# A GNN with residual layer norms: in the last stage GpSimd's two powers of a block are one instruction on 128x16 elements, for blocks three places apart

## The reference

```python
out = _ffn(h, W1u, b1u, W2u, b2u)            # h = [x, agg], 128 features to 64; two GELUs
sq = jnp.sum(out * out, axis=-1, keepdims=True)
out = out * jax.lax.rsqrt(jnp.maximum(sq, EPS_L2))
...
x = _layernorm(x + out, axis=-1)             # (x - mean) / sqrt(var + 1e-5)
```

## Time and profile before

| | |
|---|---|
| time, median of 3 runs | 2929.86 us (2928.93 to 2934.58) |
| span of the profiled execution | 2927.9 us |
| what the median adds to that span | 1.96 us |
| last stage in that span | from 2543.0 us to the end |
| busy over the whole span | PE 73%, PEld 58%, DVE 76%, ACT 36%, POOL 79% |
| mean granted TensorE clock | 0.930 |

### The profile page before, as it was taken

One profiled execution on the slowest core, in us unless ns is written; L12 is line 12 of the kernel. 1 busy time (PEld: TensorE's weight loads), 2 busy tenths in 40 slices (PEclk: granted clock), 3 DMA queues, 4 the chain that ended last, 5 costly groups with the idle time before them and its releaser, 6 DMA issues. The chain is left out here.

```text
span 2927.9 us, 40992 instructions
## 1 busy us (share of the span) xinstructions
PE 2145.7 (73%) x12594; PEld 1685.5 (58%) x12594; DVE 2220.5 (76%) x5824; ACT 1060.7 (36%) x1964; POOL 2325.4 (79%) x1770
## 2 busy tenths in 40 slices
PE   4036555555555554469999999999998989699997
PEld 3035455555454543447777777777776667466664
DVE  5069988888888886548887877777777778278988
ACT  0000000000000000025555555545554545289997
POOL 7777888888888888757788887878888887479998
PEclk9999999999999955569999999999999999699998
DMA  9888888888888767457778777777776877456664
GB/s 229 212 195 192 177 186 174 181 173 184 181 185 170 163 140 157 97 157 177 183 185 185 186 170 181 180 170 174 179 179 159 183 161 156 93 173 218 222 217 169
DMA packets 1035727, 516.39 MB, mean 176 GB/s; under 512 B 540224, under 2 KB 998000, under 8 KB 1035512
## 3 DMA queue, kind: packets, MB, share of 16 engines
q1 hardware_dynamic: 764616, 372.57, 48.0%
q0 software_dynamic: 143888, 76.97, 19.2%
q10 hardware_dynamic: 127008, 64.23, 7.6%
HBM read 269.84 MB, written 243.78 MB: 175 GB/s over the span
## 5 line engine op out<-in xcount | busy, mean ns | idle before, releaser
L304 PE MATMUL sums<-xg,weigh 128*128 128x64 f32 x1960 | 439.1, 421 | 510.1 <-ACT ms L327 366.0
L557 POOL DMA_INDIRECT state<-ms,sidx x391 | 621.8, 1590 | 146.2 <-issue 117.0
L304 PEld LDWEIGHTS sums<-xg,weigh 128*128 128x128 f32 x1960 | 424.7, 330 | 543.7 <-issue 497.6
L260 POOL DMA_INDIRECT table<-ms,sidx x391 | 617.5, 1579 | 137.4 <-issue 114.7
L372 DVE TENSOR_SCALAR weigh<-rowp,key,ew 128x128 f32<-128x128 f32 (+3 forms) x784 | 424.3, 605 | 165.4 <-PE rowp L292 157.8
L538 POOL DMA_INDIRECT box<-table,node_dst x391 | 383.3, 980 | 132.2 <-issue 112.7
L247 POOL DMA_INDIRECT xg<-in_x,node_src x391 | 379.8, 971 | 120.5 <-issue 105.7
L327 ACT ACTIVATE ms<-sums 128x256 f32<-128x256 f32 x98 | 37.6, 384 | 1142.7 <-DMA table<-ms,sidx 1017.1
L378 DVE SCALAR_TENSOR_TENSOR seen<-rowp,key,earlier 128x128 f32<-128x128 f32 (+3 forms) x784 | 383.9, 548 | 0.0
L588 PE MATMUL z_p<-turned_s,wz 128*128 128x512 f32 x588 | 326.1, 637 | 23.5 <-ACT turned_s L670 20.5
L598 PE MATMUL o_p<-cenz,leaky 128*128 128x65 f32 x2352 | 306.6, 291 | 39.6 <-DVE leaky L758 39.6
(11 more groups left out here) (97 smaller groups left out, 3552.5 us busy)
## 6 DMA issues: line engine op xcount, KB each, us to landing
box<-table SPq DMA_DIRECT2D x97, 768.0 KB, 5.2
joins<-weigh ACTq DMA_DIRECT2D x98, 640.0 KB, 3.8
weigh_in<-joins SPq DMA_DIRECT2D x98, 640.0 KB, 7.0
table<-rows SPq DMA_DIRECT2D x97, 512.0 KB, 5.3
pair<-state SPq DMA_DIRECT2D x97, 512.0 KB, 4.0
xin<-in_x SPq DMA_DIRECT2D x97, 256.0 KB, 6.1
state<-y SPq DMA_DIRECT2D x97, 256.0 KB, 7.7
out<-y SPq DMA_DIRECT2D x97, 256.0 KB, 2.2
```

The costliest lines, as they stand in the source:

```text
L260: pool.indirect_dma_start(out=table[:, :], out_offset=bass.IndirectOffsetOnAxis(ap=sidx[0][:, i:i + 1], axis=0), in_=ms[k % MR][:, b, :], ...
L304: last = pe.matmul(sums[k % 2][:, a * D:(a + 1) * D], block_of(0, k, b)[:, a * P:(a + 1) * P], xg[:, k * WT + b, :], start=b == a, stop=b ...
L557: pool.indirect_dma_start(out=state[:, :], out_offset=bass.IndirectOffsetOnAxis(ap=sidx[1][:, at:at + 1], axis=0), in_=ms[k % SM][:, b, :] ...
```

## The change

GpSimd takes both powers in one instruction. The sums of squares of block n and the sums about the mean of block n - 3 (`APART`) lie side by side in one tile `square_sums` [128, 2, 8], the results in `inverses` of the same shape, and one `tensor_tensor` with the power operation goes over 128x16 elements. For the first three and the last three of the 101 values of n only one half exists, and the instruction has 128x8 elements. One semaphore `inverted` takes the place of `inv_in` and `rstd_in`. In all there are 101 powers instead of 196: 95 of 128x16 and 6 of 128x8.

```diff
@@ -829,8 +829,9 @@
                 SP_, SY, SV = 8, 8, 4
                 pair = [sb(f"pair{s}", [P, G, 2, D], F32, c) for s in range(SP_)]
                 y = [sb(f"y2_{s}", [P, G, D], F32, c) for s in range(SY)]
-                small = {q: [sb(f"{q}2_{s}", [P, G], F32, c) for s in range(SV)] for q in ("ssq", "inv", "var", "rstd")}
-                mhalf = sb("mhalf", [P, G], F32, c)
+                square_sums = [sb(f"square_sums{s}", [P, 2, G], F32, c) for s in range(SV)]
+                inverses = [sb(f"inverses{s}", [P, 2, G], F32, c) for s in range(SV)]
+                mhalf = sb("mhalf", [P, 2, G], F32, c)
                 sq_o = [sb(f"sq_o2_{s}", [P, G, M8], F32, c) for s in range(2)]
                 sq_y = [sb(f"sq_y2_{s}", [P, G, D], F32, c) for s in range(2)]
                 turned_s = [[sb(f"turned_s2_{s}_{h}", [P, GH * P], F32, c) for h in range(2)] for s in range(2)]
@@ -845,13 +846,14 @@
                 stored = [sem(f"stored2_{s}") for s in range(SY)]
                 two = lambda name: [sem(f"{name}_{h}") for h in range(2)]
                 turned, turned_in, hid_up = two("turned2"), two("turned_in2"), two("hid_up2")
-                (half_in, preset, hid_in, out_up, out_in, cen_up, squared, summed_o, guarded_o, inv_in, scaled, added, squared_y,
-                 summed_y, guarded_y, rstd_in, normed) = (sem(f"{q}2") for q in (
-                     "half_in", "preset", "hid_in", "out_up", "out_in", "cen_up", "squared", "summed_o", "guarded_o", "inv_in", "scaled",
-                     "added", "squared_y", "summed_y", "guarded_y", "rstd_in", "normed"))
+                (half_in, preset, hid_in, out_up, out_in, cen_up, squared, summed_o, guarded_o, inverted, scaled, added, squared_y,
+                 summed_y, guarded_y, normed) = (sem(f"{q}2") for q in (
+                     "half_in", "preset", "hid_in", "out_up", "out_in", "cen_up", "squared", "summed_o", "guarded_o", "inverted", "scaled",
+                     "added", "squared_y", "summed_y", "guarded_y", "normed"))
+                APART = 3
 
                 def wide(t):
-                    return t[:, :].rearrange("p (g o) -> p g o", o=1).to_broadcast([P, G, D])
+                    return t.rearrange("p (g o) -> p g o", o=1).to_broadcast([P, G, D])
 
                 def banks(t, width):
                     return t[:, :, 0:GH * M8].rearrange("p b (g f) -> p b g f", g=GH)[:, :, :, 0:width]
@@ -886,23 +888,20 @@
 
                     @block.gpsimd
                     def _(pool):
-                        def inverse_norm(i):
-                            pool.wait_ge(guarded_o, i + 1)
-                            wait(pool, scaled, i - SV + 1)
-                            pool.tensor_tensor(small["inv"][i % SV][:, :], small["ssq"][i % SV][:, :], mhalf[:, :], ALU.pow
-                                               ).then_inc(inv_in, 1)
-
-                        def inverse_deviation(i):
-                            pool.wait_ge(guarded_y, i + 1)
-                            wait(pool, normed, i - SV + 1)
-                            pool.tensor_tensor(small["rstd"][i % SV][:, :], small["var"][i % SV][:, :], mhalf[:, :], ALU.pow
-                                               ).then_inc(rstd_in, 1)
-
-                        pool.memset(mhalf[:, :], -0.5).then_inc(half_in, 1)
+                        def inverse_roots(n):
+
+                            at = slice(0 if n < NCH else 1, 2 if n >= APART else 1)
+                            wait(pool, guarded_o, min(n + 1, NCH))
+                            wait(pool, guarded_y, n - APART + 1)
+                            wait(pool, scaled, min(n - SV + 1, NCH))
+                            wait(pool, normed, n - SV - APART + 1)
+                            pool.tensor_tensor(inverses[n % SV][:, at, :], square_sums[n % SV][:, at, :], mhalf[:, at, :], ALU.pow
+                                               ).then_inc(inverted, 1)
+
+                        pool.memset(mhalf[:, :, :], -0.5).then_inc(half_in, 1)
                         pool.wait_ge(half_in, 1)
-                        for t in range(NCH + 5):
-                            of(t, 5, inverse_deviation)
-                            of(t, 2, inverse_norm)
+                        for n in range(NCH + APART):
+                            inverse_roots(n)
 
                     @block.tensor
                     def _(pe):
@@ -995,20 +994,20 @@
                     def _(dve):
                         def sum_outputs(i):
                             dve.wait_ge(squared, i + 1)
-                            wait(dve, inv_in, i - SV + 1)
-                            dve.tensor_reduce(small["ssq"][i % SV][:, :], sq_o[i % 2][:, :, :], AX_X, ALU.add).then_inc(summed_o, 1)
+                            wait(dve, inverted, i - SV + 1)
+                            dve.tensor_reduce(square_sums[i % SV][:, 0, :], sq_o[i % 2][:, :, :], AX_X, ALU.add).then_inc(summed_o, 1)
 
                         def guard_outputs(i):
-                            ssq = small["ssq"][i % SV]
+                            ssq = square_sums[i % SV][:, 0, :]
                             dve.wait_ge(summed_o, i + 1)
-                            dve.tensor_scalar(ssq[:, :], ssq[:, :], L2_EPS, None, ALU.max).then_inc(guarded_o, 1)
+                            dve.tensor_scalar(ssq, ssq, L2_EPS, None, ALU.max).then_inc(guarded_o, 1)
 
                         def scale(i):
                             s = i % SY
-                            dve.wait_ge(inv_in, i + 1)
+                            dve.wait_ge(inverted, i + 1)
                             dve.wait_ge(cen_up, i + 1)
                             wait(dve, stored[s], 16 * (i // SY))
-                            dve.tensor_tensor(halves(y[s][:, :, :]), banks(cen_p[i % 2], D), halves(wide(small["inv"][i % SV])),
+                            dve.tensor_tensor(halves(y[s][:, :, :]), banks(cen_p[i % 2], D), halves(wide(inverses[i % SV][:, 0, :])),
                                               ALU.mult).then_inc(scaled, 1)
 
                         def add_rows(i):
@@ -1020,19 +1019,19 @@
 
                         def sum_centred(i):
                             dve.wait_ge(squared_y, i + 1)
-                            wait(dve, rstd_in, i - SV + 1)
-                            dve.tensor_reduce(small["var"][i % SV][:, :], sq_y[i % 2][:, :, :], AX_X, ALU.add).then_inc(summed_y, 1)
+                            wait(dve, inverted, i + APART - SV + 1)
+                            dve.tensor_reduce(square_sums[(i + APART) % SV][:, 1, :], sq_y[i % 2][:, :, :], AX_X, ALU.add).then_inc(summed_y, 1)
 
                         def guard_variance(i):
-                            var = small["var"][i % SV]
+                            var = square_sums[(i + APART) % SV][:, 1, :]
                             dve.wait_ge(summed_y, i + 1)
-                            dve.tensor_scalar(var[:, :], var[:, :], LN_EPS, None, ALU.add).then_inc(guarded_y, 1)
+                            dve.tensor_scalar(var, var, LN_EPS, None, ALU.add).then_inc(guarded_y, 1)
 
                         def normalize(i):
                             s = i % SY
-                            dve.wait_ge(rstd_in, i + 1)
+                            dve.wait_ge(inverted, i + APART + 1)
                             dve.wait_ge(squared_y, i + 1)
-                            dve.tensor_tensor(y[s][:, :, :], y[s][:, :, :], wide(small["rstd"][i % SV]), ALU.mult).then_inc(normed, 1)
+                            dve.tensor_tensor(y[s][:, :, :], y[s][:, :, :], wide(inverses[(i + APART) % SV][:, 1, :]), ALU.mult).then_inc(normed, 1)
 
                         for t in range(NCH + 8):
                             of(t, 6, sum_centred)
```

## The result

The changed kernel takes 2950.46 us (median of 4 runs, 2948.04 to 2953.65) against 2930.2 us before on the same chip: 1.0068 times as long, 95% interval 1.0056 to 1.0080. It is slower, by half of what I forecast: 20 us and not 42. The time lies inside my range of 2936 to 2990 us. The profiled execution spans 2948.6 us, against 2927.9.

What follows compares the result with a forecast made beforehand. TensorE was taken to bound the stage at 3.596 us; the ring with the wide power, 0.86 + 3.17 = 4.03 us, would replace it: +40.8 over 94 periods, +1.0 at the end, forecast 2971 us, range 2936 to 2990.

Steps and rivals of the forecast that it cites:

- TensorE bounds the stage at 3.596 us: Last stage before the change: TensorE is last and sets 3.596 us a block, while the other engines keep its pitch.
- faster: Rival: GpSimd bounds the last stage; relieved, the pitch falls to VectorE's 3.22 us, -35 us, to 2895 us; chance 2%.
- The second power moves into the ring guard, power, `scale`: Last stage: the second power's columns join the instruction `scale` waits for; the loop becomes 0.86 + D, 4.03 us a block.
- 0.86 us for the rest of the ring: The loop without its power: 0.59 `scale` to guard, 0.16 guard, 0.08 to the power, 0.03 until VectorE resumes.
- D: Duration of GpSimd's 128x16 power, not in the trace; taken as 3.17 us, own range 2.97 to 3.27.
- the likeliest case: Wide power costs per column, D 2.97 to 3.27 us: 2953 to 2981 us, up to 2986 with extra wait; chance 71%.
- part is fixed: Rival: 0.30 to 0.48 us of a power is fixed, D 2.79 to 2.97: +6 to +23 us, 2936 to 2953; chance 5%.
- D - 2.73: Threshold in the last stage: the loop passes TensorE's 3.596 us a block when the wide power takes over 2.73 us.
- The sum: Whole kernel: +40.8 us over 94 periods and +1.0 at the end, +41.8 together; in general 95 D - 259.3 us.
- Waits at no cost, `normalize` never later: Last stage: the wide power's extra waits taken as 0 us a period; `normalize` stands a round later than `scale`.
- TensorE with gaps, waiting at `centre`: Sign in the last stage: TensorE has gaps, waiting at `centre` or behind it, busy 3.59 of 4.03 us (89%).
- The rule of the Trainium skill: About 2.6 cycles an element on GpSimd: eight more columns cost 17 ns, D would be 1.65 us and the time unchanged.

Runs made afterwards that it cites:

- 2.59: The changed kernel with its wide power cut to 14 of 16 columns: 2926.38 us, 1.0003 of the kernel before.
- 3.28: The changed kernel with two 128x8 powers in place of the wide one, both released at the end of the second: 2976.88 us, 1.0179 of the kernel before.
- 4.17 us: The changed kernel with 24 columns in the wide power, the last eight unread constants: 3061.51 us, 1.0466 of the kernel before.
- Cutting the ring with the power untouched: The changed kernel with VectorE's guard of a block's sum issued ahead of the `scale` of the block before: 2929.32 us, 1.0015 of the kernel before.
- the run with the powers by width: The kernel before with extra powers of 1 to 32 columns and additions at the end of GpSimd's program: 2893 ns for a 16-column power.

## Why the prediction was wrong

- *TensorE bounds the stage at 3.596 us*: right. With a multiplication for the power, the time was 0.9994 of before. GpSimd as the bound (my rival "faster", -35 us) is excluded.
- *The second power moves into the ring guard, power, `scale`*: right. The lengths of the power 2.59, 2.90, 3.28 and 4.17 us gave 3.60, 3.78, 4.16 and 5.05, and each of the last three is the power's length and 0.88. Cutting the ring with the power untouched brought the time back to 0.15% above before (0.06% to 0.24%).
- *0.86 us for the rest of the ring*: 0.88 measured, since `scale` to guard is 0.61 when `scale` is the one that waits (0.59 before). Over 94 periods that is 1.9 us.
- *"I take D = 2 x 1.636 - 0.10 = 3.17 us"*: **the step that failed.** D is 2.90. I read the fixed part of a power from a memset, an instruction that reads nothing, and took 0.10 us. It is 0.37 us, beyond even the 0.30 at which I ended the likeliest case. The case "part is fixed" (2.79 to 2.97 us, 2936 to 2953 us in all) held both D and the time, and I gave it 5%, against 71% for 2953 to 2986; it should have had far more. The range was right only because it reached over this case. The error is magnified: the ring's excess over TensorE is the small difference D - 2.73, which 0.27 us less of D cut from 0.44 to 0.17.
- *The sum*: 95 x 2.90 - 259.3 = 16.2 us, plus 1.9 for the 0.88, 1.5 for a later start of the stage that no instruction of the change explains, and 1.1 for the last period of 4.14 us and the end of the stage beyond its terms: 20.7, as between the spans. The mechanism was right and one term mis-sized: D took 25.6 us of the 41.8 away (95 x 0.27), and the small terms gave 4.5 back.
- *Waits at no cost, `normalize` never later*: right, by the multiplication and by `normalize` not waiting from 2600 to 2900 us.
- *TensorE with gaps, waiting at `centre`*: half right. It is held at `centre`, by 0.19 us a period, but its busy share stays at 99% where 3.59 of 3.78 us would be 95%; only the starts show it. I had `centre` 0.4 us clear of `scale` and didn't follow that margin: it is down to 0.10 as soon as the ring sets the pitch.
- *The rule of the Trainium skill, "GPSIMD Engine Reference", section "3.1 Elementwise — side-by-side cycle accounting"*, 2.6 cycles an element, or by that page's 1.2 GHz an estimated 2.2 ns a column: here the additions rise by 243 - 211 = 32 ns over 16 columns, 2 ns each, which is near it. The power costs 158 ns a column, over 70 times as much. The page measured its figure on an add and has none for a power.

## What to carry to other kernels

Merging two instructions saves one start (0.38 us here) and makes the first one's user wait for both. Before doing it, write down the ring through the instruction and compare it with the pitch of the engine that bounds the stage: here the second power was free beside the ring, and inside it cost all that stood above the threshold. In the kernel before, the chain that ended last and a busy share of 91% pointed to an engine with slack, and who never waits was the better guide. In the changed kernel that guide fails too: TensorE is busy 99% and hardly waits, and yet the ring holds it. Starts of the same call from one block to the next, and the gap from a release to the start that it allows, showed it.

Where a threshold decides, an unknown duration should be measured before the forecast. The nearest relative would not have been near enough: an addition of 8 columns takes 194 ns, some 0.18 us of it fixed, and with that for the fixed part D would have come to 3.09 us and the loss to 34 us. Only a second width of the power itself gives the 0.37. Without it, the case of a larger fixed part deserves a large chance.

## What the runs showed of the hardware

A power on GpSimd costs 370 ns and 158 ns a column of 128 partitions from 2 to 32 columns, and 538 ns for one column behind others (the first of the row took 921). An addition of the same shape costs 194, 211 and 243 ns at 8, 16 and 32 columns.

A matmul that waits for a PSUM buffer started 0.10 or 0.11 us after the end of VectorE's instruction that frees it, in each period from 2600 to 2900 us of the runs with powers of 3.28 and 4.17 us. With the 2.90 us power TensorE's busy share (99.31%) did not show this wait.

The granted TensorE clock in the first 1000 us, before the stage that was changed, differs between executions of the same code. Before, and then after:

```profile
...
0.00:500.00 500.00, 213.65 (x964) 200.63 (x964) 344.14 (x1018) 31.06 (x67) 388.14 (x334) 1.00 0.87 195
500.00:1000.00 500.00, 276.33 (x1247) 260.00 (x1248) 424.06 (x1235) 40.53 (x90) 403.96 (x304) 1.00 0.83 177
...
```

```profile
...
0.00:500.00 500.00, 209.51 (x964) 196.71 (x964) 342.73 (x1013) 30.89 (x66) 387.76 (x334) 0.55 0.87 195
500.00:1000.00 500.00, 274.02 (x1237) 257.72 (x1237) 423.68 (x1233) 40.69 (x90) 403.62 (x304) 0.51 0.82 176
...
```

1.00 is the level of 2.4 GHz, and the 0.51 to 0.55 lie near 1.2 GHz. The run with the powers by width, whose first two stages are those of the kernel before, had 0.56 and 0.52 there, so the change isn't the reason. TensorE is busy about as long at either (213.65 and 209.51 us for 964 matmuls), and the last stage's first power starts 1.5 us apart. So either the clock level isn't what sets the time in these stretches, or the recorded level isn't the real one there; no run tells the two apart.
